# Nine halves of 4-bit codes decoded ahead of the token filters, with four masks on each of two engines, and the filtered sequence over other buffers

## The reference, cut to what matters

```python
def _L0_tok_ref(A_abslog, A_phase, C, L):          # h, length 1024 for each of 32 sequences x 64 channels
    A = jnp.exp(A_abslog + 1j * A_phase)
    dtA = jnp.log(A)
    Cc = (C[..., 0] + 1j * C[..., 1]) * (A - 1.0) / dtA
    K = jnp.exp(dtA[:, :, None] * t)
    return 2.0 * jnp.einsum('chn,hnl->chl', Cc, K).real

def dequantize_nf4(w_idx, absmax):
    w = NF4_CODE[w_idx.reshape(-1, BLOCK)] * absmax[:, None]
    return w.reshape(out_f, in_f)

h = _L0_tok_ref(L0_tok_A_abslog, L0_tok_A_phase, x, 1024)
h = h + _L0_attn_ref(_layernorm(h), Wq, Wk, Wv, Wo)
h = h + _L0_ffn_ref(_layernorm(h), w_idx, absmax, bias)     # x @ dequantize_nf4(w_idx, absmax).T + bias
h = h + _L1_attn_ref(_layernorm(h), ...)                    # convolution, selective scan of 16 states, gate
h = h + _L1_ffn_ref(_layernorm(h), ...)                     # 8 experts of rank 16, top 2, on a base matrix
```

## Time and profile before

| | us |
|---|---|
| median of 3 runs (4314.92 to 4315.89) | 4315.31 |
| the profiled execution, its own time | 4315.74 |
| its span in the trace | 4313.6 |
| PE, DVE, POOL, ACT busy over the span | 3993.6, 2792.4, 2173.6, 2016.3 |
| mean granted TensorE clock (share of the full one) | 0.966 |

### The profile page before, as it was taken

The page is one execution under the profiler, slowest core; times in us unless marked ns, Lnnn a source line. Parts: engine busy times, 40 slices in busy tenths (PEclk is TensorE's granted clock), DMA queues, the critical chain, the costliest instruction groups (busy, mean ns, idle before and its releaser), DMA issues.

```text
span 4313.6 us, 58578 instructions
## 1 busy us (share of the span) xinstructions
PE 3993.6 (93%) x22408; PEld 2615.9 (61%) x22408; DVE 2792.4 (65%) x3035; ACT 2016.3 (47%) x2958; POOL 2173.6 (50%) x912
## 2 busy tenths in 40 slices
PE   3879999899999999999999999999999999989998
PEld 1548777443667867544467867644366877744466
DVE  7745573899445474599735565399935557379953
ACT  5642344677332243677522234577633234467732
POOL 0013333788533433588733334488933333378862
PEclk7989999999999999999999999999999999999999
DMA  3332233000222223200122223300032222310021
GB/s 97 79 127 74 79 103 110 32 15 14 95 91 76 86 70 122 70 15 15 57 93 93 74 79 113 103 12 17 12 122 85 82 74 103 108 38 15 14 81 69
DMA packets 93813, 303.22 MB, mean 70 GB/s; under 512 B 11520, under 2 KB 15872, under 8 KB 91008
## 3 DMA queue, kind: packets, MB, share of 16 engines
q1 hardware_dynamic: 84352, 283.04, 19.8%
q10 hardware_dynamic: 9216, 16.78, 1.0%
HBM read 255.74 MB, written 44.04 MB: 69 GB/s over the span
## 4 chain that ended last, share of the span: by engine, by line
PE 50%; issue 29%; DVE 9%; POOL 9%; ACT 2%; DMA 0%; POOLq 0%; DVEq 0%; ACTq 0%
PE psg L908 20%; PE psx L1148 10%; POOL sb_wl L521 9%; PE psg L1163 8%; DVE sb_wst L1690 6%; PE psg L976 3%; PE psg L1177 2%; PE psg L981 1%; PE psg L1125 1%; PE psx L1190 1%; PE psg L1174 1%; PE psg L1135 1%; DVE psg L1663 1%; DVE psg L1662 1%; PE psg L1272 0%
## 5 line engine op out<-in xcount | busy, mean ns | idle before, releaser
L521 POOL TENSOR_TENSOR sb_wl<-sb_raw,sb_wh 128x1024 fp32r<-128x1024 f32 x388 | 966.0, 2494 | 1929.7 <-ACT sb_wh L619 1929.6
L1690 DVE TENSOR_TENSOR_SCAN sb_wst<-sb_dA,psx 128x1024 f32<-128x1024 f32 x512 | 1140.6, 2271 | 39.2 <-ACT sb_dA L751 23.7
L1148 PEld LDWEIGHTS psx<-sb_dgB,sb_duT 64*128 64x128 f32 x4096 | 360.1, 190 | 526.3 <-DVE sb_wst L1690 258.4
L751 ACT ACTIVATE sb_dA<-sb_dlt,sb_a_sb 128x504 f32<-128x504 f32 x1024 | 646.4, 705 | 59.8 <-DVE sb_wst L1690 54.2
L1148 PE MATMUL psx<-sb_dgB,sb_duT 64*128 64x256 f32 x4096 | 593.2, 410 | 85.5 <-DVE sb_wst L1690 83.7
L619 ACT ACTIVATE sb_wh<-sb_raw 128x1024 fp32r<-128x1024 f32 x388 | 407.0, 1053 | 537.4 <-PE psg L908 192.9
L554 POOL TENSOR_TENSOR sb_wst<-sb_wst,sb_cb_lo 128x1024 f32<-128x1024 f32 x256 | 599.5, 2365 | 90.7 <-DVE sb_wst L1690 90.4
L554 POOL TENSOR_TENSOR sb_wst<-sb_wst,sb_cb_hi 128x1024 f32<-128x1024 f32 x256 | 598.5, 2358 | 77.6 <-DVE sb_wst L1690 77.6
L1163 PE MATMUL psg<-sb_wst,sb_cst 64*64 64x512 f32 x4096 | 562.1, 621 | 10.3 <-POOL sb_wst L554 9.6
L908 PE MATMUL psg<-sb_xh,sb_wh 128*128 128x512 f32 x2112 | 556.1, 407 | 15.3 <-DVE sb_qs L1598 11.5
L908 PE MATMUL psg<-sb_xh,sb_wl 128*128 128x512 f32 x2112 | 525.8, 391 | 0.0
(11 more groups left out here) (275 smaller groups left out, 4993.3 us busy)
## 6 DMA issues: line engine op xcount, KB each, us to landing
sb_raw<-in_w SPq DMA_DIRECT2D x360, 512.0 KB, 3.5
sb_raw<-w_ffn_dequantized SPq DMA_DIRECT2D x32, 512.0 KB, 3.2
gates<-sb_gt ACTq DMA_DIRECT2D x64, 256.0 KB, 2.4
sb_gin<-gates SPq DMA_DIRECT2D x64, 256.0 KB, 2.6
...
```

What stands on the lines that cost most here:

```text
L521: pool.tensor_tensor(rest(b, i0), raw[:, i0 % RAW, :, :], high(b, i0).bitcast(F32), ALU.subtract).then_inc(s_wl, 1)
L751: ins_ = A(dA[:, (m * NQ + k) % RING, :, n, 1:S], dlt[:, m % 2, :].rearrange("p (b s) -> p b s", b=NB)[:, :, 1:S], ACT.Exp, scale=a_sb[:, ...
L1148: ins_ = mm(psx[:, 2 * j + r, :].rearrange("p (a t e) -> p a t e", a=8, e=2)[:, :, :, e], duT[r0:r0 + 64, m % 2, i * P:(i + 1) * P], dgB[r ...
L1690: v.tensor_tensor_scan(wst[:, x, 4 * j:4 * j + 4, :, :].rearrange("p b n s -> p (b n s)"), dA[:, x, 4 * j:4 * j + 4, :, :].rearrange("p b ...
```

## The change

The diff, cut to its core:

```diff
-BY_ACT = 3
-BY_DVE = PAIRS - BY_ACT
-RING_ACT, RING_DVE = 2, 3
+RING_ACT, RING_DVE = 3, 4
-EARLY = 5
-LATE = [[5, 6], [7], [8, 9], [10], [11, 12], [13], [14], [15]]
+EARLY = 9
+LATE = [[9], [10], [11], [12], [13], [14], [15], []]
+BY_ACT = [4 if i < EARLY else 3 for i in range(HALVES)]
+BY_DVE = [PAIRS - n for n in BY_ACT]
+ACT0 = [sum(BY_ACT[:i]) for i in range(HALVES + 1)]
+DVE0 = [sum(BY_DVE[:i]) for i in range(HALVES + 1)]
...
         with ExitStack() as c:
+            ah = sb("ah", [P, KC, T], F32R, c)
+            al = sb("al", [P, KC, T], F32R, c)
             xc = sb("xc", [P, KC, T], F32, c)
             xh = sb("xh", [P, KC, T], F32R, c)
             xl = sb("xl", [P, KC, T], F32R, c)
-            ah = sb("ah", [P, KC, T], F32R, c)
-            al = sb("al", [P, KC, T], F32R, c)
...
-                if i + 2 < HALVES:
-                    sp.wait_ge(s_dqf, i + 1)
-                    load_codes(i + 2)
...
+            def converted(i):
+                q = i % 2
+                act.wait_ge(s_dqi[q], i // 2 * 32 + 32)
+                if i >= 2:
+                    act.wait_ge(s_mkd, DVE0[i - 1])
+                A(dqf[:, q, :, :], dqi[:, q, :, :], ACT.Copy).then_inc(s_dqf, 1)
+                if i + 2 < HALVES:
+                    act.wait_ge(s_dqf, i + 1)
+                    load_codes(act, i + 2)
+            def masks(i):
+                if i == 0:
+                    converted(0)
+                if i + 1 < HALVES:
+                    converted(i + 1)
                 act.wait_ge(s_dqf, i + 1)
...
             masks(0)
+            masks(1)
             A(tab[:, 0, :, :], tab[:, 0, :, :], ACT.Sin, bias=0.0).then_inc(s_tabA, 1)
-            masks(1)
+            masks(2)
             A(tab[:, 1, :, :], tab[:, 1, :, :], ACT.Sin, bias=0.0).then_inc(s_tabA, 1)
-            masks(2)
+            masks(3)
             A(tabs[:, :, :, :], tabs[:, :, :, :], ACT.Sin, bias=0.0).then_inc(s_tabA, 1)
+            masks(4)
             A(gco[:, 0:2, :], gco[:, 0:2, :], ACT.Sin).then_inc(s_tabA, 1)
             A(etab[:, :, :], etab[:, :, :], ACT.Exp).then_inc(s_tabA, 1)
...
+                            if b == 0 and j == 1:
+                                act.wait_ge(s_keep, 32)
                             A(ah[:, j - 1, :], ao[:, :, :].rearrange("p b s -> p (b s)"), ACT.Copy).then_inc(s_ah, 1)
...
             def masks(i):
+                if i >= 2:
+                    weights(i - 2)
                 for j in range(BY_DVE[i]):
...
-                if i >= 1:
-                    weights(i - 1)
...
                     if L == 0:
-                        v.wait_ge(s_keep, 32)
                         v.wait_ge(s_cst, 16 * 6)
```

More of the change, by code:

```diff
@@ L262, in tower @@
         with ExitStack() as c:
-            sb("over_x", [P, 3 * KC, T], F32, c)
+            lb = [sb(f"lb{n}", [P, KC, P], F32R, c) for n in range(2)]
             wT = sb("wT", [P, T], F32, c)
@@ L275, in tower @@
             cb_hi = sb("cb_hi", [P, 2, NB, 4, S], F32, c)
+            dgB = sb("dgB", [P, XT, NQ, 2, 4, 32], F32, c)
             wst = sb("wst", [P, RING, NB, 4, S], F32, c)
@@ L287, in tower @@
         with ExitStack() as c:
+            sb("over_ah", [P, KC, T], F32, c)
             yh = sb("yh", [P, DC, T], F32R, c)
             yl = sb("yl", [P, DC, T], F32R, c)
-            lb = [sb(f"lb{n}", [P, KC, P], F32R, c) for n in range(2)]
         psg = ctx.enter_context(nc.psum_tensor("psg", [P, 4, 512], F32))
@@ L387, in loop, with load_codes @@
             return eng.Fori(0, n)
+        def load_codes(eng, i):
+            m, q = i // 2, i % 2
+            for c in range(2):
+                eng.dma_start(dqi[64 * c:64 * c + 64, q, :, :],
+                              ins["w_idx"][m].rearrange("(r p) x -> p r x", r=2)[:, :, q * HALF:(q + 1) * HALF]).then_inc(s_dqi[q], 16)
         @block.sync
@@ L394, in _ @@
             sp.dma_start(cst[:, :], ins["const"]).then_inc(s_mode, 16)
-            def load_codes(i):
-                m, q = i // 2, i % 2
-                for c in range(2):
-                    sp.dma_start(dqi[64 * c:64 * c + 64, q, :, :],
-                                 ins["w_idx"][m].rearrange("(r p) x -> p r x", r=2)[:, :, q * HALF:(q + 1) * HALF]).then_inc(s_dqi[q], 16)
             def load_absmax(i):
@@ L565, in _ @@
             act.wait_ge(s_mode, 80)
-            def masks(i):
+            def converted(i):
                 q = i % 2
@@ L606, in _ @@
             A(gco[:, 2, :], mode[:, 0, :], ACT.Exp).then_inc(s_tabA, 1)
-            for i in range(3, EARLY):
+            for i in range(5, EARLY):
                 masks(i)
@@ L867, in codes @@
                     return ins_
-                for j in range(BY_DVE):
-                    at = i * BY_DVE + j
+                for j in range(BY_DVE[i]):
+                    at = DVE0[i] + j
                     pe.wait_ge(s_mkd, at + 1)
                     codes(j, mkd[:, at % RING_DVE, :, :], j == 0, False).then_inc(s_usedd, 1)
-                for j in range(BY_ACT):
-                    at = i * BY_ACT + j
+                for j in range(BY_ACT[i]):
+                    at = ACT0[i] + j
                     pe.wait_ge(s_mka, at + 1)
-                    codes(BY_DVE + j, mka[:, at % RING_ACT, :, :], False, j == BY_ACT - 1).then_inc(s_useda, 1)
+                    codes(BY_DVE[i] + j, mka[:, at % RING_ACT, :, :], False, j == BY_ACT[i] - 1).then_inc(s_useda, 1)
             def filters(g):
@@ L1371, in reduce_turns @@
                 own.link(ts(dst, dst, PI_IN, -PI_IN, ALU.min, ALU.max))
+            masks(0)
             own.link(tt(reg, ph.unsqueeze(2).to_broadcast([P, S, 32]),
@@ L1414, in _ @@
                 own.link(tt(tabs[:, t, :, :], tabs[:, t, :, :], etabs[:, :, :], ALU.mult))
-            masks(3)
+            masks(5)
             v.wait_ge(s_tabA, 7)
@@ L1439, in _ @@
                 own.link(stt(g2, gim, C("gmix", 4 * e + 3, 1), g2, ALU.mult, ALU.add))
-            masks(4)
+            masks(6)
             v.wait_ge(s_x, 64)
@@ L1451, in _ @@
                 own.link(tt(coef[:, e, :, :], coef[:, e, :, :], x, ALU.add))
+            masks(7)
             def powers(g):
@@ L1474, in _ @@
             powers(0)
+            masks(8)
             for g in range(S // FG):
@@ L1479, in _ @@
                     masks(i)
-            weights(HALVES - 1)
+            for i in range(HALVES - 2, HALVES):
+                weights(i)
             def newton(own, var, eps, r0, tmp, r):
@@ L1620, in _ @@
                             v.wait_ge(s_ao, b * KC + j)
+                            if b == 0 and j == 1:
+                                v.wait_ge(s_keep, 32)
                             tt(al[:, j - 1, :], ao[:, :, :].rearrange("p b s -> p (b s)"), ah[:, j - 1, :].bitcast(F32),
```

20 lines of the change are left out of this document (9 added, 11 removed).

## The result

| | before | after |
|---|---|---|
| median, us (runs) | 4315.31 (4313.85 to 4315.89) | 4291.82 (4287.02 to 4297.04, 5 runs) |
| span of the profiled execution, us | 4313.6 | 4289.7 |
| mean granted clock | 0.966 | 0.966 |

The account below looks back on a forecast made before the run. DVE came nearest to bounding up to the first filters, then PE to the first mean. From 4315.74, less 22.7 at the mean and 1.2 at the end, 4291.8; less 0.4 for the median, rounded to 4291.5, range 4285 to 4300.

Parts of the forecast that it names:

- ACT up to the exponentials, 81.7: ACT's start, tables, six conversions, six pairs of issues and 20 masks end at 81.7 us, where it was 73.3.
- The rule against this part: Issuing loads from ACT brings no bandwidth; with loads kept on SP, ACT's sum would end 5 to 10 us earlier.
- DVE and PE to the first filters, 134.1: From the exponentials on, DVE's tables and halves 7 and 8 bring the first filters at 134.1 us, 16.7 later than before.
- the loop named: Before the first filters, ACT's last mask of half 7 needs a ring slot, so PE must first use 30 matmuls: 121.1 us.
- Filters, 92.5: From first filters to first mean, eight groups and seven halves take 92.5 us against 131.9; first mean at 226.6.
- The thin cover: In each group ACT needs 11.3 us and DVE 11.4 beside PE's 11.9, half a microsecond to spare.
- The rival in which a group stays at 13.05: ACT or DVE bounds the filter groups, which stay at 13.05 us: 8 us more, 4299.5; 8 in 100.
- The end, 1.2: SP no longer waits for the last decoded half's store before its first strip: 1.2 us gained.
- the filtered sequence, 0: In block 0, centre's earlier start gains 0, since strip 2's load hides it; upper bound 7.1 us.
- PE at the higher level ahead of the filters: Half 7's 30 matmuls run at 2.4 GHz, 3.3 us instead of 6.4: 4288.5; 12 in 100.
- Stalling issues: Each issue of codes stalls on ACT, a pair costs 4.2 us: 4325, slower; 3 in 100.
- The change doesn't do what it says: The prologue ends earlier and block 0 gives it back at a transfer: within 8 us of 4315; 2 in 100.

Follow-up runs that it names:

- r9_loads_sp: The changed kernel with the loads of codes back on SP, so ACT issues no transfer: 4284.22 us, ratio 0.9931 to the kernel before.
- r1_again: The changed kernel a second time with no edit, with a second profiled execution: 4289.21 us, ratio 0.9948 to the kernel before.
- r5_old_rings: The changed kernel with the old rings, RING_ACT, RING_DVE = 2, 3: 4305.01 us, ratio 0.9978 to the kernel before.
- r3_old_buffers: The changed kernel with the old buffers and the wait for s_keep ahead of centre again: 4288.65 us, ratio 0.9944 to the kernel before.
- r4_strips_first: The changed kernel with strips 2 and 3 loaded ahead of the three stores of hT: 4271.60 us, ratio 0.9911 to the kernel before.
- r6_strips_first_old_buffers: The changed kernel with strips 2 and 3 ahead of the stores, but the old buffers: 4295.37 us, ratio 0.9954 to the kernel before.

## Why the prediction was right, and where it was not

*What bounds the kernel.* The two stretches and their bounds were read rightly, but one step was left out: I put down to ACT's ring of two only the wait of 0.66 us in the late groups. Its 28.5 us ahead of the exponentials stand in the same trace, and so does their sum with the later ones, second in the list of all waits up to 290 us:

```profile
ACT sb_mka L583 <- PE psx L865: 88.0, 13, 26.2
```

The prediction's own prices would have shown it. For the kernel before they give 9.7 + 1.3 + 3 x 1.07 + 9 x 2.23 + 10.7 = 45.0 us up to the products, where it was 73.3; the missing 28.3 are those waits. So the sum nowhere says that the rings carry the gain. It priced the new order with the new rings in it, which was right for the total, and hid that the order loses with them.

*ACT up to the exponentials, 81.7.* Measured 87.08 and 80.89. Masks, conversions, tables and pairs together were 69.6 to 70.0 us, where I had 72.0, and none of it was a wait for the ring. A pair was 1.26 of issue and 1.25 by r9_loads_sp; I took 1.5. The term that was missing is a wait for codes: "No load of codes is waited for before" was true of the kernel before, and I carried it over to a kernel that asks for the codes of half 2 while the constants and `x` are being loaded: 1.1 us of later start and 6.2 of waiting in one execution, 1.5 in the other. That ACT takes DVE's place was right: DVE was there at 87.08 - 19.86 = 67.2, forecast 67.

*The rule against this part.* Half 2's codes were there at 30.8 when ACT issued them and at 30.6 when SP did, but by 24.9 in r1_again, where ACT issued them too, so the landing differs more between executions than between issuers. The issues cost ACT 7.3 to 7.7 us. The Trainium skill ("DMA: Bandwidth & Descriptors", Rules for kernel authors) says that spreading issues over engines adds no bandwidth. The traces agree: up to the first filters 106 and 110 GB/s moved with ACT as an issuer, 112 with SP alone. The 5 to 10 us that I gave for loads on SP were 7.

*DVE and PE to the first filters, 134.1.* 137.86 and 132.78. From the products to there 50.8 and 51.9 us, forecast 52.4, by the loop named: half 7 on PE at 119.91 (87.08 and 32.8; I had 31.8 and 1.2 for it), ACT's `Relu` of half 7's last mask stands 1.80 us for PE (3.49 in r1_again), and ACT's last mask of half 8 comes just ahead of the filters.

*Filters, 92.5.* 91.8 and 93.4. The period was 11.98 against 11.9. The thin cover held. The rival in which a group stays at 13.05 was not an idle one: r5_old_rings shows it to the hundredth, so only the rings kept it away. The first group took 7.17, the lower of its two bounds, and 8.86 in r1_again, near the upper.

*The end, 1.2, and the filtered sequence, 0.* 1.24 by SP's rows, and 0 by r3_old_buffers. The cover that I named for the buffers, strip 2, is confirmed by r4_strips_first and r6_strips_first_old_buffers; the 7.1 us that I gave as their upper bound was too small a view, since the cover itself could be moved and 12 to 14 us lay beneath it.

*The sum.* In the profiled execution the first mean was 3.0 us later than forecast and block 0's first layer 2.9 shorter at a higher clock. The 4291.82 is near the forecast because these cancel. In r1_again the first mean is at 226.22, 0.4 from the forecast, and block 0 as before; its time is 4289.21 with a kernel before at 4311.07, which is 21.9 us, forecast 23.8. The path through the prologue held, the reason for its gain was incomplete, and a single total to 0.3 us was luck.

*The rivals.* PE at the higher level ahead of the filters: in part. The stretch has 0.73 and 0.79 of the clock, but halves 7 and 8 each began at a granted clock of 0.50 (119.91 to 122.00, 130.56 to 132.60) and ended at 1.00 (124.07 to 126.60, 134.50 to 137.86). From half 7's first matmul to the mask of ACT that it holds back it took 5.1 us, and 6.2 in r1_again, where the forecast has 6.4 and the rival 3.3. Stalling issues: no, 1.26 to 1.53 a pair. The change doesn't do what it says: block 0 gave nothing back.
